# Local attention of a fused transformer kernel in units of four heads instead of two, with the softmax division moved behind the product with the values

## The reference, cut to what matters

```python
qkv = shift_token(x) @ wqkv             # 8 heads of 64 for each of q, k, v
q, k = l2norm(q) * q_scale, l2norm(k) * k_scale
q, k = rotary_xpos(q, k)
# local attention: a query sees the keys at most WINDOW=64 back, none ahead
sim = where(mask, -max, einsum(q * 8, k))
out = softmax(sim) @ v
x = x + out @ wo
x = x + feed_forward(layer_norm(shift_token(x)))   # gelu-gated
```

## Time and profile before

| what | us |
|---|---|
| median of 3 runs (863.97 to 866.32) | 864.89 |
| the profiled execution | 870.1 |
| its span, first to last instruction | 868.2 |
| TensorE, VectorE, ScalarE, GpSimd busy in the span | 660.7, 614.3, 532.1, 152.5 |
| share of the chain that ended last: PE, DVE, ACT, waiting for nothing shown | 47%, 32%, 12%, 7% |

### The profile page before, as it was taken

How to read it: one execution, slowest core, us unless ns; L and a number is a source line. 1 busy time by engine, 2 the same in 40 slices (tenths; PEclk the granted TensorE clock), 3 DMA queues, 4 the chain that set the end, 5 groups by cost and what they waited for, 6 DMA issues and landing times.

```text
span 868.2 us, 13186 instructions
## 1 busy us (share of the span) xinstructions
PE 660.7 (76%) x4636; PEld 403.9 (47%) x4636; DVE 614.3 (71%) x1349; ACT 532.1 (61%) x1237; POOL 152.5 (18%) x169
## 2 busy tenths in 40 slices
PE   2469961845889889768999997948888795779866
PEld 1212230532556557534555554434556553446545
DVE  7772347357998886677667664799775569996764
ACT  4479977454779888144656663835565466556752
POOL 5030040012678667511000000000000000000000
PEclk9669985775555555768999998968999798799998
DMA  9300000000000000000000000000000000000000
GB/s 301 124 1 1 1 2 0 1 0 1 1 2 2 2 2 2 1 0 1 2 1 1 1 2 1 1 0 1 1 2 1 0 1 1 0 1 2 1 1 24
DMA packets 9060, 10.56 MB, mean 12 GB/s; under 512 B 2746, under 2 KB 7844, under 8 KB 8868
## 3 DMA queue, kind: packets, MB, share of 16 engines
q1 hardware_dynamic: 8996, 9.73, 3.4%
HBM read 9.21 MB, written 0.52 MB: 11 GB/s over the span
## 4 chain that ended last, share of the span: by engine, by line
PE 47%; DVE 32%; ACT 12%; issue 7%; DMA 0%; POOL 0%; ACTq 0%; DVEq 0%
PE ps L1378 5%; PE ps L1628 4%; PE ps L1510 4%; PE ps L1608 4%; PE ps L1592 3%; DVE s_nmB L1020 3%; DVE s_nmD L1299 2%; ACT arena L506 2%; PE ps L1435 2%; PE ps L1593 2%; PE ps L1407 2%; PE ps L1366 2%; ACT arena L544 2%; PE ps L1703 2%; PE ps L1789 2%
## 5 line engine op out<-in xcount | busy, mean ns | idle before, releaser
L374 POOL TENSOR_SCALAR arena<-arena,s_rB,s_zpu 128x512 uint8<-128x512 f32 x128 | 98.7, 787 | 63.3 <-DVE s_rB L993 62.3
L544 ACT ACTIVATE arena<-ps,s_nmB 128x512 f32<-128x512 f32 x128 | 86.6, 688 | 23.4 <-DVE s_nmB L1020 23.2
L566 ACT ACTIVATE arena<-ps,s_nmx 128x512 f32<-128x512 f32 (+3 forms) x128 | 60.7, 528 | 63.6 <-DVE s_nmx L1118 63.2
L1113 DVE TENSOR_REDUCE s_nmx<-ps 128x1 f32<-128x512 f32 (+3 forms) x128 | 56.6, 484 | 37.7 <-PE ps L1593 37.2
L1020 DVE TENSOR_REDUCE s_nmB<-ps 128x2 f32<-128x1024 f32 x64 | 77.2, 1217 | 7.3 <-PE ps L1496 7.0
L1510 PE MATMUL ps<-ident,arena 128*128 128x128 f16 x512 | 59.1, 308 | 8.0 <-ACT arena L536 7.5
L506 ACT ACTIVATE arena<-ps 128x1024 f32<-128x1024 f32 x64 | 60.9, 1026 | 7.0 <-PE ps L1419 6.8
L1510 PEld LDWEIGHTS ps<-ident,arena 128*128 128x128 f16 x512 | 51.3, 143 | 21.4 <-POOL arena L374 20.3
L633 ACT ACTIVATE sq<-ps,s_nbD,s_dq 128x192 f32<-128x192 f32 (+1 forms) x64 | 31.3, 493 | 36.2 <-DVE s_nbD L1303 36.2
L1496 PE MATMUL ps<-staged 8*128 8x512 f16 x128 | 45.2, 593 | 10.4 <-ACT arena L544 9.5
L1770 PE MATMUL ps<-arena 128*64 128x128 f32 x448 | 40.4, 297 | 10.5 <-ACT arena L646 9.5
(11 more groups left out here) (341 smaller groups left out, 1533.9 us busy)
## 6 DMA issues: line engine op xcount, KB each, us to landing
vec<-in_vec SPq DMA_DIRECT2D x1, 1882.0 KB, 11.7
w_d<-in_wqkv SPq DMA_DIRECT2D x2, 768.0 KB
vec<-in_vec SPq DMA_DIRECT2D x1, 960.0 KB, 8.2
w_h<-in_w SPq DMA_DIRECT2D x2, 341.0 KB
x_tok<-in_x SPq DMA_DIRECT2D x1, 512.0 KB, 4.0
arena<-in_w_f SPq DMA_DIRECT2D x2, 256.0 KB, 7.6
rope<-in_rope SPq DMA_DIRECT2D x1, 512.0 KB, 10.4
w_do<-in_wo SPq DMA_DIRECT2D x2, 256.0 KB
```

Source lines behind the costliest of these rows:

```text
L374: nc.gpsimd.tensor_scalar(u8[:, n % 4, j, :, 0], prob[:, n % 2, j * 512:j * 512 + 512], sm("rB", 8)[:, c:c + 1], sm("zpu", H)[:, h:h + 1], ...
L544: nc.scalar.activation(prob[:, n % 2, j * 512:j * 512 + 512], ps[:, j, :], ACT.Exp, bias=sm("nmB", 8)[:, c:c + 1], accum_out=sm("sumB", 8) ...
L566: nc.scalar.activation(probC[:, n % 2, at(qt):at(qt) + w], ps[:, bank, col:col + w], ACT.Exp, bias=nmx[:, TB * b + qt, h:h + 1]).then_inc( ...
L1113: ins = V.tensor_reduce(nmx[:, TB * b + qt, h:h + 1], ps[:, bank, col:col + P * (qt + 1)], X, ALU.max, negate=True)
```

## The change

A unit is now one tile and four heads: 16 units in a layer instead of 32, and one loop over both batches. The parts:

1. `scores`: four heads fill two banks; the mask is added for two heads by one matmul. `maxima`: one reduction for four heads, whose result is kept in PSUM (`nm`), beside the scores.
2. `exps`: four exponentials without an accumulated sum; the probabilities aren't divided. `turn_p` turns them, 8 transposes; the copy of the turned ones is shared, two heads on ScalarE, two on VectorE (`copy_pt`).
3. `values`: the turned probabilities are now the loaded weights, 128 columns, and the values stream, 65 columns: each head of `vD` has a column of ones behind its 64, which gives the row's sum. The output has queries on partitions. `put_o` takes the reciprocal of the sums and divides the 4 x 64 outputs; `turn_o` turns these by two transposes, ScalarE copies them (`copy_ot`).
4. `project_o` and `add_o` go tile by tile, inside the loop, two iterations behind.
5. The evacuation of the projection is two instructions, for q and k and for v.
6. The queries of batch 1 are rotated by GpSimd (8 instructions, 2 of 1024 and 2 of 512 elements for each half of the batch), the keys still by VectorE: 8 steps, two in each of the iterations 3 to 6.
7. `turn_qk(1)` is taken apart: its groups alternate with the transposes, values and output transposes of the last units of batch 0 (iteration u = 8).
8. The layer norm of batch 0 lies at iterations 11 to 17.

The diff, cut to its core (`U` is the unit's number over both layers):

```diff
-qkvD = carve([T, 3 * INNER], start=0)
+qkvD = carve([T, 2 * INNER + DH * (DHD + 1)], start=0)
+vD = qkvD[:, :, 2 * INNER:].rearrange("p t (h c) -> p t h c", h=DH)
...
-a = (wide["sq"], wide["dev"])[U // 2 % 2][:, 4 * (U % 2):4 * (U % 2) + 4, :]
-return a.rearrange("p t c -> p (t c)").rearrange("p (j k) -> p j k", j=2)
+return wide[("sq", "dev")[U % 2]][:, :, :].rearrange("p t c -> p (t c)").rearrange("p (j k) -> p j k", j=4)
...
+def score_banks(u):
+return ps[:, 6 * (u % 2):6 * (u % 2) + 2, :].rearrange("p r (j k) -> p r j k", j=2)
+def outside_d(t):
+return P if t % TB == 0 else WINDOW
...
+for l in range(DEPTH):
+    pool.wait_ge(sem["g_mm" if l else "ocn"], T * l if l else B)
+    nc.gpsimd.memset(vD[:, :, :, DHD:DHD + 1], 1.0).then_inc(sem["v_ones"], 1)
+    r1 = o_tok[:, :, :].rearrange("p t c -> p (t c)").rearrange("p (t h c) -> p t h c", t=2, h=DH)
+    r2 = staged[:, :, :].bitcast(F32).rearrange("p a b -> p (a b)").rearrange("p (t h c) -> p t h c", t=2, h=DH)
+    pool.wait_ge(sem["d_sq"], T * (l + 1))
+    pool.wait_ge(sem["rope0"], 2 * (l + 1))
+    for t in (TB, TB + 2):
+        step(rope_terms(nc.gpsimd, t, 2, 0, r1, r2, step), "rope1Q")
...
-        nc.scalar.activation(qkvD[:, t, :], ps[:, k:k + 3, :].rearrange("p a b -> p (a b)"), ACT.Copy)\
+        nc.scalar.activation(qkvD[:, t, 0:2 * INNER], ps[:, k:k + 2, :].rearrange("p a b -> p (a b)"), ACT.Copy)
+        nc.scalar.activation(vD[:, t, :, 0:DHD], ps[:, k + 2, :].rearrange("p (h c) -> p h c", h=DH), ACT.Copy)\
...
+    def exps(u):
+        t, half = divmod(u, 2)
+        k0 = outside_d(t)
+        act.wait_ge(sem["maxD"], U + 1)
+        if U >= 2:
+            act.wait_ge(sem["ptD"], 2 * (U - 1))
+        for j in range(4):
+            h = DH * t + 4 * half + j
+            c = 4 * (u % 2) + 2 * (j % 2) + j // 2
+            nc.scalar.activation(prob_d(U)[:, j, k0:256], score_banks(u)[:, j % 2, j // 2, k0:256], ACT.Exp,
+                                 scale=sm("dq8", 8 * T)[:, h:h + 1], bias=sm("nbD", 8)[:, c:c + 1])\
+                .then_inc(sem["expD"], 1)
+    def copy_pt(u):
+        k0 = outside_d(u // 2) // P * P
+        act.wait_ge(sem["ptD"], 2 * U + 1)
+        if U >= 2:
+            act.wait_ge(sem["pvD"], U - 1)
+        nc.scalar.activation(probTD[:, u % 2, 0:2, k0:256],
+                             ps[:, 2, :].rearrange("p (j k) -> p j k", j=2)[:, :, k0:256], ACT.Copy)\
+            .then_inc(sem["ptcD"], 1)
+    def copy_ot(u):
+        t, half = divmod(u, 2)
+        act.wait_ge(sem["otD"], U + 1)
+        if T * l + t >= 2:
+            act.wait_ge(sem["do_mm"], T * l + t - 1)
+        nc.scalar.activation(oTD[:, t % 2, 2 * half:2 * half + 2, :],
+                             ps[:, 4 + u % 2, 0:256].rearrange("p (a b) -> p a b", a=2), ACT.Copy)\
+            .then_inc(sem["otcD"], 1)
+    for u in range(2 * T + 3):
+        if u == 2 * TB:
+            turned_qk(1, 0)
+            copy_pt(u - 1)
+            turned_qk(1, 2)
+            copy_ot(u - 3)
+            turned_qk(1, 4)
+            turned_qk(1, 6)
+        if u < 2 * T:
+            exps(u)
+        if 1 <= u <= 2 * T and u != 2 * TB:
+            copy_pt(u - 1)
+        if u == 14:
+            squares_d(0)
+        if u == 2 * T:
+            roots_d(0)
+        if u >= 3 and u != 2 * TB:
+            copy_ot(u - 3)
...
+    def add_o(t):
+        dve.wait_ge(sem["do_mm"], T * l + t + 1)
+        step(V.tensor_tensor(f[:, t, :], f[:, t, :], ps[:, 5, 384:512], ALU.add), "do_ev")
...
+    def maxima(u):
+        t, half = divmod(u, 2)
+        k0 = outside_d(t)
+        dve.wait_ge(sem["sD"], U + 1)
+        if U >= 2:
+            dve.wait_ge(sem["expD"], 4 * (U - 1))
+        nb = sm("nbD", 8)[:, 4 * (u % 2):4 * (u % 2) + 4].rearrange("p (r j) -> p r j", r=2)
+        nm = ps[:, 6 * (u % 2), 0:4].rearrange("p (r j) -> p r j", r=2)
+        step(V.tensor_reduce(nm, score_banks(u)[:, :, :, k0:256], X, ALU.max, negate=True))
+        hh = DH * t + 4 * half
+        free(V.tensor_tensor(nb, nm, dq8[:, hh:hh + 4].rearrange("p (j r) -> p r j", r=2), ALU.mult), "maxD")
+    def copy_pt(u):
+        k0 = outside_d(u // 2) // P * P
+        dve.wait_ge(sem["ptD"], 2 * U + 2)
+        if U >= 2:
+            dve.wait_ge(sem["pvD"], U - 1)
+        free(V.tensor_copy(probTD[:, u % 2, 2:4, k0:256],
+                           ps[:, 3, :].rearrange("p (j k) -> p j k", j=2)[:, :, k0:256]), "ptcD_V")
+    def put_o(u):
+        o = ps[:, 4 + u % 2, 0:4 * (DHD + 1)].rearrange("p (j c) -> p j c", j=4)
+        rs = sm("rsD", 8)[:, 4 * (u % 2):4 * (u % 2) + 4]
+        dve.wait_ge(sem["pvD"], U + 1)
+        recip(rs, o[:, :, DHD])
+        if U >= 2:
+            dve.wait_ge(sem["otD"], U - 1)
+        free(V.tensor_tensor(oD[:, u % 2, :, :], o[:, :, 0:DHD], per_row(rs, DHD), ALU.mult), "o_D")
     rest = late_rope()
-    for b in range(B):
-        for u in range(TB * 4 + 1):
...
-    normalise(0)
-    add_o(1)
+    for u in range(2 * T + 4):
+        if u == 2 * TB:
+            turned_qk(1, 1)
+            copy_pt(u - 1)
+            turned_qk(1, 3)
+            put_o(u - 2)
+            turned_qk(1, 5)
+            turned_qk(1, 7)
+        if u < 2 * T:
+            maxima(u)
+        if 3 <= u < 2 * TB:
+            next(rest, None)
+        if u >= 5 and u % 2:
+            add_o((u - 5) // 2)
+        if u == 2 * TB + 3:
+            send(0)
+        if u == 2 * TB + 4:
+            receive(l, 0)
+        if 1 <= u <= 2 * T and u != 2 * TB:
+            copy_pt(u - 1)
+        if 3 <= u < 2 * TB:
+            next(rest, None)
+        if 2 <= u < 2 * T + 2 and u != 2 * TB:
+            put_o(u - 2)
+        if u == 2 * TB + 4:
+            less_mean(0)
+        if u == 2 * T - 1:
+            variance(0)
+        if u == 2 * T + 1:
+            normalise(0)
+    send(1)
...
+    def scores(u):
+        t, half = divmod(u, 2)
+        k0 = outside_d(t)
+        if u % (2 * TB) == 0:
+            pe.wait_ge(sem["qk_evA"], 4 * (B * l + u // (2 * TB) + 1))
+            pe.wait_ge(sem["qk_evV"], 4 * (B * l + u // (2 * TB) + 1))
+        if U >= 2:
+            pe.wait_ge(sem["expD"], 4 * (U - 1))
+        for j in range(2):
+            for r in range(2):
+                M(score_banks(u)[:, r, j, k0:256], qTD[64 * r:64 * r + 64, 2 * half + j, t * P:(t + 1) * P],
+                  kTD[64 * r:64 * r + 64, 2 * half + j, (t - 1) * P + k0:(t + 1) * P],
+                  start=(j == 0), stop=False)
+        for r in range(2):
+            ins = M(score_banks(u)[:, r, :, k0:256], identb[:, :],
+                    dmask[:, k0:256].unsqueeze(1).to_broadcast([P, 2, 256 - k0]), start=False, stop=True)
+        ins.then_inc(sem["sD"], 1)
...
+    def turn_p(u):
+        if U < 2:
+            pe.wait_ge(sem["outside"], 2)
+        for j in range(4):
+            if j % 2 == 0:
+                pe.wait_ge(sem["expD"], 4 * U + j + 2)
+                if U >= 1:
+                    pe.wait_ge(sem["ptcD_V" if j else "ptcD"], U)
+            for k in range(outside_d(u // 2) // P, 2):
+                c = 256 * (j % 2) + P * k
+                ins = nc.tensor.transpose(ps[:, 2 + j // 2, c:c + P], prob_d(U)[:, j, P * k:P * k + P], ident)
+            if j % 2:
+                ins.then_inc(sem["ptD"], 1)
+    def values(u):
+        t, half = divmod(u, 2)
+        if u == 0:
+            pe.wait_ge(sem["v_ones"], l + 4)
+        if U >= 2:
+            pe.wait_ge(sem["otcD"], U - 1)
+        if u % 2 and t >= 1:
+            pe.wait_ge(sem["do_ev"], T * l + t)
+        if u == 2 * TB + 2:
+            pe.wait_ge(sem["shift_ev"], B * l + 1)
+        ks = range(outside_d(t) // P, 2)
+        for j in range(4):
+            if j % 2 == 0:
+                pe.wait_ge(sem["ptcD_V" if j else "ptcD"], U + 1)
+            for k in ks:
+                c = (DHD + 1) * j
+                ins = M(ps[:, 4 + u % 2, c:c + DHD + 1], probTD[:, u % 2, j, P * k:P * k + P],
+                        vD[:, t - 1 + k, 4 * half + j, :], start=(k == ks[0]), stop=(k == 1))
+        ins.then_inc(sem["pvD"], 1)
+    def turn_o(u):
+        pe.wait_ge(sem["o_D"], U + 1)
+        for i in range(2):
+            ins = nc.tensor.transpose(ps[:, 4 + u % 2, P * i:P * i + P],
+                                      oD[:, u % 2, 2 * i:2 * i + 2, :].rearrange("p j c -> p (j c)"), ident)
+        ins.then_inc(sem["otD"], 1)
     def project_o(t):
-        pe.wait_ge(sem["o_D"], T * l + TB * (t // TB) + TB)
+        pe.wait_ge(sem["otcD"], 2 * T * l + 2 * t + 2)
         for c in range(4):
-            ins = M(ps[:, 5 - t // TB, (t % TB) * P:(t % TB) * P + P], oTD[:, c, t * P:(t + 1) * P],
-                    w_do[:, l, c, :], start=(c == 0), stop=(c == 3))
+            ins = M(ps[:, 5, 384:512], oTD[:, t % 2, c, :], w_do[:, l, c, :], start=(c == 0), stop=(c == 3))
...
+    turn_ready(0)
+    for i in range(8):
+        turn_qk(0, i)
+    for u in range(2 * T + 4):
+        if u == 2 * TB:
+            turn_ready(1)
```

(25 more changed lines are left out.)

248 lines of the change are left out of this document (60 added, 188 removed).

## The result

The changed kernel takes 858.58 us (median of 6 runs, 857.62 to 859.22) against 866.10 for the kernel before in the same comparison: ratio 0.9907, 95% interval 0.9882 to 0.9932, faster by 7.5 us. The profiled execution took 857.62 us with a span of 855.8.

A forecast was written before the change was run, and what follows sets the result against it. VectorE was taken to bound batch 0, TensorE batch 1. A layer gains 6.7 - 1.0 - 0.3 = 5.4, less 0.3 for semaphores: 5.1, two layers 10.2 us, so a median of 855 us, range 844 to 865.

The forecast's parts named there:

- Values at the pace of the loads: TensorE, values of a four-head unit: loading 128 columns sets the pace, 16 records at 0.11, 1.75 us.
- VectorE's unit: VectorE's work for four heads (maxima, scaling, copy, reciprocal, division, gaps, adding o every second unit): 2.6 us.
- ScalarE's exponentials: ScalarE, four exponentials of 192 without the sum: 1.35 us instead of 2.0.
- The wait in unit 5: Batch 0, TensorE: `values(3)` waits for tile 0's addition behind maxima and a rotation step; 8.4 us from scores to scores.
- The transition: Between the batches, TensorE alternates turning q and k with the last unit's work: 6.7 us, then a last copy, 0.9.
- The evacuation in two instructions: Projection, ScalarE: 0.15 us more a tile, hidden by VectorE except for the first two tiles; 0.3 us lost a layer.
- The gain of batch 0: Layer 2: batch 1 starts at 783.1 instead of 789.8, 6.7 us gained, with GpSimd's rotation costing 0.
- rival B: Batch 0: GpSimd's late rotation holds VectorE's rotation instructions, about 10 us; 871 us, slower than before; chance 0.10.
- Maxima in PSUM at 0: VectorE: keeping the maxima in PSUM costs 0 a unit, bounds -0.02 to +0.06 us.
- Batch 1: TensorE: units 8 to 15 take 34.0 us, the end 10.4; 44.6 in all instead of 43.6, 1.0 us lost.
- Rival C: Batch 1's end and waits eat the gain: 3.5 us lost instead of 1.0; 860.5 to 862 us; chance 0.16.
- Rival D: Granted clock falls to 1.2 GHz for 5 us more of a layer: 865 us, no change; chance 0.10.

The follow-up runs named there:

- after_again: The changed kernel run once more, unaltered, beside the kernel before: 859.74 us, ratio 0.9925 to the kernel before.
- values_96: The changed kernel with each values matmul streaming 96 columns instead of 65: 860.36 us, ratio 0.9927 to the kernel before.
- factors_psum: The changed kernel with batch 1's factors worked on in PSUM and copied back to SBUF: 854.63 us, ratio 0.9865 to the kernel before.
- root_and_add: The changed kernel with batch 1's root and factors in PSUM and `add_o` ahead of the rotation step: 851.09 us, ratio 0.9830 to the kernel before.
- pairs_pool: The kernel before, units of two heads kept, with only batch 1's queries rotated by GpSimd: 868.04 us, ratio 1.0038 to the kernel before.
- tail_banks: The changed kernel with the last two tiles projected into banks 2 and 3, last values before tile 6's projection: 856.21 us, ratio 0.9889 to the kernel before.

## Why the prediction was right, and which steps were not

The forecast was 855 us and the range 844 to 865; the time is 858.58, and against 866.10 the change gave 7.5 us where I had 10.2 (6.1 in after_again). The side, the exchange between the batches and the range held; GpSimd's part was not free, as I had it. Step by step:

**Values at the pace of the loads: right.** I took 16 x 0.11 = 1.75 for a unit; measured 1.74, and values_96 shows that streaming isn't what sets it.

**VectorE's unit: right.** Maxima of 768 elements 0.97 (0.96), the copy 0.69 (0.69), reciprocal 0.18 (0.19), division 0.42 (0.42), the small product from PSUM 0.16.

**ScalarE's exponentials: off, without consequence.** Four take 1.72 us where I said 1.35: 0.40 from start to start without the sum, against 0.50 with it. ScalarE is busy 23.07 of 46.41 us in batch 1.

**The wait in unit 5: right in kind.** `values(3)` waits for the addition behind a rotation step: 1.69 us on TensorE (at 755.43), and from the scores of unit 5 to those of unit 6 8.0 us pass (749.55 to 757.55) for 8.4.

**The transition: right.** From the first turned q and k on TensorE at 767.16 to batch 1's first scores 7.3 us, against 6.7 + 0.9.

**The evacuation in two instructions: right in size.** With the clock alike, the stretches from the first projection to the first scores are 0.1 and 0.2 us longer in after_again than before (38.0 and 69.9), for 0.3.

**The gain of batch 0: the step that failed, the cost of nothing for GpSimd.** "The GpSimd rotation ... Cost 0, cover 25 us." Its durations and its end were right (15.0 us, over at 738.8 before the first key rotation at 744.12, which took 1.22), and rival B, as I put it, didn't come. But I looked for collisions only among VectorE's rotations. GpSimd started at 723.78 and ran over the two TENSOR_SCALAR of `factors(1)`, each with one SBUF input, which none of my rows showed beside it: 0.45 + 1.60 = 2.05 us in front of the first maxima. I had the scores of unit 3 end 8.0 us behind the stretch's start, so start at about 6.6; they started at 10.8, and at 6.8 in factors_psum, without the hold. So the step down to unit 3 was right but for it. The 4.0 us are TensorE's longer gap (2.67 for 0.94) and records at the lower clock: from the first transposes to the scores of unit 3 6.1 us (735.56 to 741.65), 3.9 in root_and_add (733.77 to 737.63). Batch 0 gave 4.2 to 5.1 for the 6.7. The hold is not all of it: in factors_psum the stretch is 42.2, still 1.1 over the forecast's 41.1 (742.0 to 783.1), with the lower clock behind `values(3)` (9.45 us for the work that takes 6.24), where the forecast had 0.4 a layer for the clock. In layer 2 the 5.0 us that root_and_add takes off are the shorter first gap, 1.7, those 2.2 of clock and the shorter wait for `add_o`, 1.3: 5.2, to 0.2 us. The Trainium skill, "SBUF — State Buffer", section "Who interferes with whom", which I had drawn on for two-input instructions alone, says in the same place that `tensor_scalar`, `copy` and `cast` can take VectorE's second pair of ports too, and then contend; the trace agrees (0.18 became 0.63 and 1.78). It also says that `tensor_reduce` never contends on this chip; the trace agrees (the maxima, 0.70 beside GpSimd).

**Maxima in PSUM at 0: right by its own price, incomplete in what it is for.** It costs nothing, and it keeps the small product clear of GpSimd; with the maxima and the division in SBUF (pairs_pool) GpSimd's part made the kernel slower.

**Batch 1: the sum right, the tail short.** Units 8 to 15 took 34.1 us (774.48 to 808.53) for 34.0. The tail took 12.4 (808.53 to 820.89) for 10.4. 1.2 of the 2.0 are the lower clock (the last projection, for one, 2.08 at 817.27 for 1.16). The rest is about the 0.7 that tail_banks gives back: I had the projection of tile 6 and `values(15)` back to back, 2.7 for both, but the values wait for that tile's addition too, since they share its bank, and start 1.6 us behind the projection's start instead of 0.95 (812.00 to 813.59). At the full clock batch 1 takes 45.2 us (both layers of after_again) where it took 43.6 before at the full clock: 1.6 lost for the 1.0 forecast.

**Rival C: refuted as the main loss.** TensorE is busy 42.15 of 46.41 us in batch 1 (91%), not under 85%. **Rival D: partly true.** The clock in batch 0 is 0.96 and 0.92, where before had 0.89 and 0.93, so it did not fall; but the same work gets 1.00 without the two waits, and 2.2 of 5.0 us in layer 2 are that.

**Luck.** The six executions compared with 866.10 all lie at 857.6 to 859.2; four of the twelve of after_again lie at 863.1 to 863.6, so a draw of those would have come closer to the range's end of 865. Two sums on record are slightly off: 775.4 + 7.6 is 783.0, not 783.1, and rival C's loss of 3.5 instead of 1.0 leaves 2.6 us a layer, 859.7, not 860.5 to 862.

## What to carry to other kernels

When work moves to GpSimd, lay its whole run in time over VectorE's instructions and ask of each, also those of 0.2 us, whether its operands are in SBUF: a small one at the head of the chain can cost most (here 2 us held, and 2 more by the clock behind it). Moving its operand to PSUM took the hold away here; starting GpSimd later only moved the hold to the key rotations. Moving the pair, which batch 0 doesn't need, behind the first maxima was not tried. When two waits stand in one stretch of TensorE (here 16 to 20 us apart), take them away together before judging either: alone they gave 0 to 1.4 us a layer, together 5.0.

## What the runs showed of the hardware

A TENSOR_SCALAR of 32 f32 elements a partition, SBUF to SBUF, was held 1.6 us by one GpSimd multiplication; a reciprocal of 64 elements in SBUF beside the same one was not (0.55 both times). A product of 2 elements from two SBUF operands was held (0.16 became 0.82 and 0.96) as one of 1024 was (1.22 became 2.70).

TensorE's time at 1.2 GHz did not add up over the two gaps of batch 0. With a wait of 1.69 us alone it was 7 us in a layer, with one of 2.7 alone 7 and 10, with both 3 to 7, and with 0.94 and 0.43 none (four layers). The same wait was followed by the lower level in one layer and not in another: in the changed kernel the 2.7 of layer 1 and the 1.69 of layer 2 were not.

An f32 matmul behind a load of 128 columns took 0.109 us a record at the full clock with 65 streamed columns and 0.110 with 96.

An exponential of 192 elements repeats every 0.40 us without a running sum and every 0.50 with it.

A GpSimd product of 1024 f32 elements took 2.35 us and of 512 1.27 where no VectorE instruction held it; VectorE's of the same sizes took 1.22 and 0.68.
